# Turning the adjacency mask of a two-layer graph kernel with VectorE squares and DMA instead of TensorE transposes and ScalarE copies

## The reference, cut to what matters

```python
# x: (8192, 128), adj: (8192, 8192) of 0 and 1, all float32
h = relu(layernorm(x))
# first layer: attention over the neighbours
Wh = h @ W
e = leaky_relu(Wh @ a1 + (Wh @ a2).T, 0.2)
att = softmax(where(adj > 0, e, -9e15), axis=-1)
x = x + relu(att @ Wh)
# second layer: sum of messages over the neighbours
h = relu(layernorm(x))
node = h @ W1                                   # (8192, 16)
hw = einsum('nc,kcf->nkf', h, W2)
msg = einsum('nk,nkf->nf', node, hw)
x = x + relu(adj @ msg + node @ b)
```

## Time and profile before

| | |
|---|---|
| median of 3 runs | 1871.63 us |
| lowest and highest | 1871.55 and 1872.37 us |
| the profiled execution | 1872.76 us |
| its span | 1871.2 us |
| granted clock of TensorE, mean | 0.993 |
| instructions | 38399 |
| DMA | 452.24 MB, mean 242 GB/s |

### The profile page before, as it was taken

One profiled execution on the slowest core, in us unless ns is written; L12 is line 12 of the kernel. 1 busy time (PEld: TensorE's weight loads), 2 busy tenths in 40 slices (PEclk: granted clock), 3 DMA queues, 4 the chain that ended last, 5 costly groups with the idle time before them and its releaser, 6 DMA issues.

```text
span 1871.2 us, 38399 instructions
## 1 busy us (share of the span) xinstructions
PE 1831.2 (98%) x13404; PEld 1590.1 (85%) x13404; DVE 1209.9 (65%) x1511; ACT 1330.3 (71%) x2144; POOL 714.5 (38%) x530
## 2 busy tenths in 40 slices
PE   7799999999999999999999999999999999999998
PEld 4699989889889888988988888898877788888886
DVE  6666677677767767777776776776656543443534
ACT  4666788877878787887788778878465655555554
POOL 0300056546546655654665564565535400000000
PEclk9899999999999999999999999999999999999999
DMA  9488967776776776777777677674753344445430
GB/s 332 154 311 320 352 243 283 289 276 265 287 288 251 295 290 251 288 284 274 271 287 278 263 292 280 251 295 156 309 198 144 141 161 161 154 159 205 152 157 22
DMA packets 105812, 452.24 MB, mean 242 GB/s; under 512 B 6736, under 2 KB 15136, under 8 KB 87968
## 3 DMA queue, kind: packets, MB, share of 16 engines
q1 hardware_dynamic: 86720, 356.53, 51.2%
q10 hardware_dynamic: 12208, 75.62, 9.9%
q0 software_dynamic: 6832, 19.41, 2.8%
HBM read 364.46 MB, written 87.07 MB: 241 GB/s over the span
## 4 chain that ended last, share of the span: by engine, by line
PE 91%; DVE 3%; ACT 2%; issue 2%; SPq 1%; DMA 1%; DVEq 0%; ACTq 0%
PE ot_ps L806 47%; PE mt_ps L850 13%; PE ot_ps L850 13%; PE hw_ps L770 11%; PE mt_ps L738 6%; ACT wh_mask L505 1%; PE h_ps L765 1%; DVE att L947 1%; DMA adj_sb<-in_adj_dram 1%; SPq L283 1%; DVE p_sb L971 1%; DVE p_sb L897 1%; ACT prod L571 1%; DVE keep L952 0%; PE h_ps L777 0%
## 5 line engine op out<-in xcount | busy, mean ns | idle before, releaser
L806 PE MATMUL ot_ps<-wh_mask,p_sb 128*128 (+1 forms) x8192 | 980.6, 277 | 5.8 <-DVE p_sb L971 5.8
L971 DVE SCALAR_TENSOR_TENSOR p_sb<-zb,qcol,mt 128x1024 f32<-128x1024 uint8 (+1 forms) x512 | 780.6, 1555 | 263.3 <-ACT mt L517 212.2
L806 PEld LDWEIGHTS ot_ps<-wh_mask,p_sb 128*128 128x128 f32 x8192 | 942.3, 192 | 7.7 <-issue 5.9
L378 POOL TENSOR_TENSOR prod<-prod 128x1024 f32<-128x1024 f32 (+2 forms) x192 | 408.0, 2125 | 516.5 <-ACT prod L571 500.6
L505 ACT ACTIVATE wh_mask<-adj_sb 128x2048 uint8<-128x2048 f32 x256 | 492.9, 1928 | 3.3 <-DMA adj_sb<-in_adj_dram 2.2
L632 ACT ACTIVATE mask<-adj_sb 128x1024 fp32r<-128x1024 uint8 x240 | 255.4, 1065 | 176.5 <-PE ot_ps L850 176.4
L517 ACT ACTIVATE mt<-mt_ps 128x1024 uint16<-128x1024 uint16 x256 | 267.5, 1046 | 151.8 <-PE mt_ps L738 150.5
L1009 DVE CAST mask<-adj_sb 128x1024 fp32r<-128x1024 uint8 x272 | 202.3, 750 | 248.5 <-PE mt_ps L850 246.6
L571 ACT ACTIVATE prod<-hw_ps,node 128x128 f32<-128x128 f32 x1024 | 278.8, 385 | 92.1 <-PE hw_ps L770 92.1
L850 PE MATMUL mt_ps<-mask,msgs 128*128 128x512 f32 x1024 | 283.0, 398 | 4.3 <-issue 3.4
L850 PE MATMUL ot_ps<-mask,msgs 128*128 128x512 f32 x1024 | 275.6, 391 | 0.8
(11 more groups left out here) (112 smaller groups left out, 612.5 us busy)
## 6 DMA issues: line engine op xcount, KB each, us to landing
adj_sb<-in_adj_dram SPq DMA_DIRECT2D x128, 2048.0 KB, 8.4
maskT_d<-mt ACTq DMA_DIRECT2D x64, 1024.0 KB, 5.2
adj_sb<-maskT_d SPq DMA_DIRECT2D x32, 2048.0 KB, 7.7
keep_d<-keep POOLq DMA_DIRECT2D x64, 128.0 KB, 6.0
p_sb<-keep_d SPq DMA_DIRECT2D x4, 2048.0 KB, 12.2
msg_d<-msg POOLq DMA_DIRECT2D x56, 128.0 KB, 5.9
msgs<-msg_d SPq DMA_DIRECT2D x7, 1024.0 KB, 10.2
wh_mask<-in_x_dram SPq DMA_DIRECT2D x8, 512.0 KB, 7.3
```

Of the source, the lines that this page charges most:

```text
L378: pool.tensor_tensor(prod[:, 0:n, :], prod[:, 0:n, :], prod[:, n:2 * n, :], ALU.add)\
L806: ins = pe.matmul(ot_ps[h][:, (t - t0) * ROW:(t - t0 + 1) * ROW], p_sb[:, r, t * P:(t + 1) * P], rows, start=False, stop=end and t == t1 - 1)
L971: dve.scalar_tensor_tensor(p_sb[:, r, :], zbf[:, bass.ds((ib % 2) * BLK, BLK)], qcol[:, bass.ds(tile + b_, 1)], mtb[:, p, k, :, b_], ALU.m ...
```

## The change

Everything that turned the mask on PE and ACT is gone: `turn_mask`, `evict`, the store from ACT and the banks' part in it. In its place:

- The rows of a block are numbered anew. A row is (y, p, b) with y = 0, 1, partition p and b = 0 to 3, so that four neighbouring columns of `adj`, four mask bytes or one 32-bit word, belong to one partition of the turned mask.
- `turn_squares` on DVE (one instruction a block of work) transposes the block's mask words within squares of 32 partitions by 32 words, from `m8` (now one place) to `sq` (the other place's room). It writes them as (square, row partition, tile), so that each square's words of one partition are 256 in a row, 1 KB; the write step is 8 words.
- `turn_back` on SP moves `sq` to `maskT_d` by four DMAs of 32 partitions each, in pieces of 1 KB, which puts every square on its right partition; waits until they have landed; and loads the block back into `mt` (1 MB, pieces of 4 KB). DVE waits for that load (`mt_in[p]`) at the start of each block of work.
- The order of the columns of `p_sb`, `zbf` and `yT` is (partition, tile) and no longer (tile, partition). PE therefore reads its weights for L806 and for the transposes of `yT` with a step of 8 fp32 words (32 bytes): `p_t`, `yT_t`. The first row of `zbf` is copied into that order, and the others come from DRAM in it.
- The mask bytes are read by `weigh` and `convert` with a step of 4 bytes, before 2.
- On ACT, `cast` waits for `squared` in place of `turned`, its four casts of a block stand at k = 0 and 1, and before the loop the casts of the first two blocks are made in the setup.
- `p_ready` starts at READY = 32, so that the waits of the first blocks are for positive numbers.

```diff
-    adj_v = adj.rearrange("(i p t) n -> i p t n", p=P, t=T)
-    x_v = x.rearrange("(i p t) f -> i p t f", p=P, t=T)
-    out_v = out.rearrange("(i p t) f -> i p t f", p=P, t=T)
-
-    zrow_d = nc.dram_tensor("zrow_d", [NT, P], FP32).ap()
-    maskT_d = nc.dram_tensor("maskT_d", [NB, NB, P, C * BLK], U16).ap()
+    SQ = 32
+    A = P // SQ
+    Y = T // 4
+    adj_v = adj.rearrange("(i y p b) n -> i p y b n", y=Y, p=P, b=4)
+    x_v = x.rearrange("(i y p b) f -> i p y (b f)", y=Y, p=P, b=4)
+    out_v = out.rearrange("(i y p b) f -> i p y (b f)", y=Y, p=P, b=4)
+
+    zrow_d = nc.dram_tensor("zrow_d", [NB, P, T], FP32).ap()
+    maskT_d = nc.dram_tensor("maskT_d", [NB, NB, Y, P, A, T * SQ], FP32).ap()
...
-        mt = sb("mt", [P, 2, C, BLK], U16)
+        mt = sb("mt", [P, 2, Y, BLK])
...
-        m8 = wh_mask[:, NT * (D + 2):].bitcast(U8).rearrange("p (s t n) -> p s t n", s=2, t=T)
-        mtb = mt[:, :, :, :].rearrange("p s c n -> p (s c n)").bitcast(U8)\
-            .rearrange("p (s c n b) -> p s c n b", s=2, c=C, b=2)
+        m8 = wh_mask[:, NT * (D + 2):NT * (D + 2) + BLK * T // 4].bitcast(U8).rearrange("p (t n) -> p t n", t=T)
+        m8w = wh_mask[:, NT * (D + 2):NT * (D + 2) + BLK * T // 4].rearrange("p (t c s) -> p t c s", t=T, s=SQ)
+        sq = wh_mask[:, NT * (D + 2) + BLK * T // 4:].rearrange("p (c w) -> p c w", w=T * SQ)
+        sq_t = wh_mask[:, NT * (D + 2) + BLK * T // 4:].rearrange("p (c r t) -> p t c r", t=T, r=SQ)
+        mtb = mt[:, :, :, :].rearrange("p s y n -> p (s y n)").bitcast(U8)\
+            .rearrange("p (s y n b) -> p s y n b", s=2, y=Y, b=4)
...
+        yT_t = yT.rearrange("p (i c t) -> p i t c", i=2, t=T)
+        p_t = p_sb[:, :, :].rearrange("p s (c t) -> p s t c", t=T)
...
+        READY = 4 * T
...
+            def turn_back(i, ib, jg, p):
+                n = 2 * i + p
+                block = maskT_d[bass.ds(2 * jg + p, 1), bass.ds(ib, 1), :, :, :, :]
+                sp.wait_ge(squared, n + 1)
+                sp.sem_inc(past_sp, 1)
+                for a in range(A):
+                    sp.dma_start(block[:, :, :, :, a, :].rearrange("j i y (x s) w -> (j i s) (y x) w", s=SQ),
+                                 sq[a * SQ:(a + 1) * SQ, :, :]).then_inc(sq_stored, 16)
+                sp.wait_ge(sq_stored, 16 * A * (n + 1))
+                sp.sem_inc(past_sp, 1)
+                sp.wait_ge(p_ready, READY + T * (n - 1))
+                sp.sem_inc(past_sp, 1)
+                sp.dma_start(mt[:, p, :, :], block.rearrange("j i y p a w -> (j i p) y (a w)")).then_inc(mt_in[p], 16)
 
             def turn(i, ib, jg, finish, last):
                 for p in range(2):
                     for h in range(2):
                         q = 2 * p + h
                         sp.wait_ge(adj_cast[q], i)
-                        sp.dma_start(adj_sb[:, q, :].rearrange("p (t n) -> p t n", n=BLK),
-                                     adj_v[bass.ds(ib, 1), :, h * HT:(h + 1) * HT,
-                                           bass.ds((2 * jg + p) * BLK, BLK)].rearrange("i p t n -> (i p) t n"))\
+                        sp.dma_start(adj_sb[:, q, :].rearrange("p (b n) -> p b n", n=BLK),
+                                     adj_v[bass.ds(ib, 1), :, h, :, bass.ds((2 * jg + p) * BLK, BLK)]
+                                     .rearrange("i p b n -> (i p) b n"))\
                           .then_inc(adj_in[q], 16)
-
-            attention_loop(sp, turn)
-
+                    if not isinstance(jg, int) or jg > 0:
+                        turn_back(i - 1, ib, jg - 1, p)
+                    elif not (isinstance(ib, int) and ib == 0):
+                        turn_back(i - 1, ib - 1, IT - 1, p)
+
+            attention_loop(sp, turn, alone=True)
+            for p in range(2):
+                turn_back(NB * IT - 1, NB - 1, IT - 1, p)
...
-            def cast(q, part, count, turned_before):
+            def cast(q, part, count):
 
                 act.wait_ge(adj_in[q], 16 * count)
-                act.wait_ge(turned, turned_before)
+                if part == 0 and q % 2 == 0 and not (q == 0 and isinstance(count, int) and count == 1):
+                    act.wait_ge(squared, 2 * (count - 1) + q // 2)
                 t = q % 2 * HT + part * (HT // 2)
-                ins = act.activation(m8[:, q // 2, t:t + HT // 2, :].rearrange("p t n -> p (t n)"),
+                ins = act.activation(m8[:, t:t + HT // 2, :].rearrange("p t n -> p (t n)"),
                                      adj_sb[:, q, part * (HT // 2) * BLK:(part + 1) * (HT // 2) * BLK], ACT.Copy,
                                      scale=EDGE)
                 if part == 1:
                     ins.then_inc(adj_cast[q], 1)
 
-            def evict(chunk, k, p, use):
-
-                act.wait_ge(turned, chunk + 1)
-                if k == 0 and not (isinstance(use, int) and use == 0):
-                    act.wait_ge(p_ready, T * (2 * use + p - 1))
-                    act.wait_ge(mt_stored[p], 16 * use)
-                act.activation(mt[:, p, k, :], mt_ps[k % 2][:, :].bitcast(U16), ACT.Copy).then_inc(evicted, 1)
...
-                if i:
-                    cast(*ahead[i - 1], 1, 0)
-            evict(0, 0, 0, 0)
-            evict(1, 1, 0, 0)
+                if 1 <= i <= 4:
+                    cast((i - 1) // 2, (i - 1) % 2, 1)
+            for q in (2, 3):
+                for part in range(2):
+                    cast(q, part, 1)
...
+                        if k < 2 and not last:
+                            for part in range(2):
+                                cast(2 * p + k, part, i + 2)
...
-            def turn_mask(chunk, k, p, casts):
-
-                if k == 0:
-                    for h in range(2):
-                        pe.wait_ge(adj_cast[2 * p + h], casts)
-                if not (isinstance(chunk, int) and chunk < 2):
-                    pe.wait_ge(evicted, chunk - 1)
-                words = mt_ps[k % 2][:, :].bitcast(BF16)
-                for t in range(T):
-                    ins = pe.transpose(words[:, t * P:(t + 1) * P],
-                                       m8[:, p, t, :].bitcast(BF16)[:, k:BLK // 2:C], ident16[:, :])
-                ins.then_inc(turned, 1)
-
             pe.wait_ge(hT_done, 2 * NB)
-            turn_mask(0, 0, 0, 1)
-            turn_mask(1, 1, 0, 1)
...
-                                                    p_sb[:, r, t * P:(t + 1) * P], rows, start=False, stop=end and t == t1 - 1)
+                                                    p_t[:, r, t, :], rows, start=False, stop=end and t == t1 - 1)
...
-                                           yT[:, (4 * g + j) * P:(4 * g + j + 1) * P], ident[:, :])
+                                           yT_t[:, g // 2, 4 * (g % 2) + j, :], ident[:, :])
...
+            def turn_squares(n, p, count):
+                for h in range(2):
+                    dve.wait_ge(adj_cast[2 * p + h], count)
+                if not (isinstance(n, int) and n == 0):
+                    dve.wait_ge(sq_stored, 16 * A * n)
+                dve.transpose(sq_t, m8w).then_inc(squared, 1)
+
+            turn_squares(0, 0, 1)
...
-                                         qcol[:, bass.ds(tile + b_, 1)], mtb[:, p, k, :, b_],
+                                         qcol[:, bass.ds(tile + b_, 1)], mtb[:, p, k // 2, :, 2 * (k % 2) + b_],
...
-                        dve.wait_ge(evicted, c + 1)
+                        if k == 0 and not (last and p == 1):
+                            turn_squares(n + 1, 1 - p, i + 1 + p)
+                        if k == 0:
+                            dve.wait_ge(mt_in[p], 16 * (i + 1))
```

99 lines of the change are left out of this document (33 added, 66 removed).

## The result

The changed kernel takes 2763.49 us (median of 4 runs, 2762.98 to 2765.13), the kernel before beside it 1872.00 us (1871.55 to 1872.57): a ratio of 1.4764, with a 95% interval of 1.4742 to 1.4786. The change costs 891 us. The prediction had 2606 us and a range that ended at 2710.

The account below looks back on a forecast made before the run. TensorE was taken to bound the loop, its weight loads running back to back. 1872.8 - 112 (transposes) + 836 (stepped weight loads) + 3 + 6 (start and end) = 2606 us, with an 8-in-10 range of 1850 to 2710.

Parts of the forecast that it names:

- The transposes go: On TensorE, 254 groups of L738's transposes at 0.44 us each leave the path: 112 us less.
- The step in the weight loads: TensorE's 8192 loads of L806 read words 32 bytes apart: 102 ns more each, 836 us; chance 0.49.
- The factor of 1.7 to 2.0: Slowdown of stepped fp32 reads on DVE (1.7) and ACT (2.0), applied to L806's weight loads: 2417 to 2699 us.
- the upper bound: Most that the step could add to one L806 weight load: a full second slot per element, 113.4 ns.
- The other end: Skill page's rule for TensorE weight loads: time set by number of columns alone, so the step adds nothing.
- DVE's turn: DVE's 64 turns of 2048 mask words: 2.2 to 4.4 us a block, hidden beside TensorE, counted as nothing.
- The mask's way through DRAM: SP's stores, wait and mask load: cycle 19.0 to 21.4 us a block, hidden under TensorE's 31.4, counted as nothing.
- the case without the step: Rival: weight loads keep 113.4 ns and transfers on SP's queue bind the attention loop, 1983 us; chance 0.27.
- ACT's evictions, start and end: 256 ACT evictions beside TensorE gain nothing; casts after the last projection add 3 us, stepped transposes of `yT` 6 us.
- What would show it: Signs in the attention loop: loads 192 to 227 ns apart, blocks 28 to 33 us, DMA share below 0.6.

Follow-up runs that it names:

- e17: Changed kernel, words by quadrant (no weight-load step), square root ahead of later casts, queue order stores, adjacency load, mask load, other adjacency load: 1852.02 us.
- e2: Kernel before the change, with only L806's weight loads reading words 32 bytes apart: 2903.43 us.
- e3: Kernel before the change, with only L806's weight loads reading words 8 bytes apart: 1918.79 us.
- e6: Changed kernel with nodes renumbered so each mask word holds four columns of one tile and weight loads read neighbouring words: 2097.59 us.
- e1: Changed kernel with L784 reading neighbouring words as weights, not words 32 bytes apart; rows mixed between tiles: 1905.13 us.

## Why the prediction was wrong

The mechanism was right and one size was off.

- *The transposes go, -112 us.* Right as TensorE's share: nothing of L738 is left in the chain, and a block in e17 is 2.0 us shorter (1.8 were counted).
- *The step in the weight loads, 8192 x 102 ns = 836 us.* **This term failed.** It measured 122 to 126 ns a load, 999 to 1032 us; with it the sum gives 2769 to 2802 us, or 2760 to 2793 without the 9 us of start and end, and 2763 were measured. The factor of 1.7 to 2.0 came from DVE's and ACT's rows, and the upper bound, "a full second slot per element, 113.4 ns more", was taken for the most it could be. e2, in the kernel before, has 127 ns more. The other end, that the number of columns alone sets a load's time, is out as well: 128 columns took 113.4 to 240.6 ns. A factor borrowed from other engines bounds nothing on this one, and 1.9 was chosen inside 2.0 where an overshoot should have been allowed: the range ended 53 us too low. With two words in 16 bytes (e3) the same engine pays 6 ns, so a row of a smaller step, such as L738's 8 bytes, could not have told.
- *DVE's turn, 2.2 to 4.4 us, hidden.* Right here: 3.88 us, hidden. The 2.2 us held without the step in its writes (2.31 us in e6). With fast weight loads it is not hidden: in e1's first row it stands in the chain at 3.9 us a block.
- *The mask's way through DRAM, counted as nothing under a slow TensorE.* Right here. For the first row it had a cycle of 18.1 to 20.5 us, and e1 shows 19.7. That the number fits is partly luck: the cycle was added up from the bytes of a block and one latency, while e1's is DVE's turn, the issues and the landing of the stores, and the turn was not in the sum. For the case without the step it named the transfers as the bound and gave up to 1983 us; e1 took 1905, and in the later rows ACT's lump of casts set the 20.0 us, an order of four instructions that the prediction had in its hands and did not follow to the root that stands behind it.
- *ACT's evictions, start and end, 0 and +9 us.* No run tested the evictions by themselves. DVE's first weights start at 79.50 us, before at 79.14: 0.4 us later, not 3. After the last weight load begins (2239.7 us) 523.8 us pass, before 523.4 (1347.8 us): the 6 us for `yT` do not show.
- *What would show it.* Loads spaced 192 to 227 ns: 235 to 239. Chunk 6.2 to 7.3 us: 7.52. Blocks of 28 to 33 us: 34.1. All three lie above their ranges, by the same term. DMA share under 0.6 in the loop: 0.56. DVE waiting for TensorE: 892.4 us.
